# Cross attention on one Trainium2 core: value and query products split into three products of parts, and products ordered by their stationary operand

## The reference, cut to what matters

```python
x = layer_norm(x, ln_m_g, ln_m_b)             # the context, 4 x 512 x 128
lat = layer_norm(latents, ln_l_g, ln_l_b)     # the normed x, 4 x 256 x 128
q = lat @ Wq                                  # 16 heads of 64
kv = concatenate([x, lat], 1) @ Wkv           # 768 keys
k, v = split(kv)
attn = softmax(q @ k.T * scale)
return (attn @ v) @ Wout
```

## Time and profile before

| | us |
|---|---|
| median of 3 runs | 1062.45 |
| lowest, highest | 1061.57, 1063.77 |
| the profiled execution: its time | 1061.55 |
| the profiled execution: its span | 1059.4 |
| TensorE busy in the span (matmuls) | 979.9 |
| loads of stationary operands (PEld) | 800.9 |
| VectorE, ScalarE, GpSimd busy | 685.9, 573.2, 176.3 |

### The profile page before, as it was taken

The page is one execution under the profiler, slowest core; times in us unless marked ns, Lnnn a source line. Parts: engine busy times, 40 slices in busy tenths (PEclk is TensorE's granted clock), DMA queues, the critical chain, the costliest instruction groups (busy, mean ns, idle before and its releaser), DMA issues.

```text
span 1059.4 us, 22196 instructions
## 1 busy us (share of the span) xinstructions
PE 979.9 (92%) x7108; PEld 800.9 (76%) x7108; DVE 685.9 (65%) x1715; ACT 573.2 (54%) x1511; POOL 176.3 (17%) x291
## 2 busy tenths in 40 slices
PE   5899979999999999999997999979999888888888
PEld 3677768888888888888884877768999665555665
DVE  5878666556666555666635788853222699999673
ACT  3676556555555555555531677745444376666440
POOL 3434120000000000000002333200000234443100
PEclk9999989999999999999998999999999899999995
DMA  6000000000000000000000000010110000000000
GB/s 254 1 1 0 1 1 1 1 1 1 0 0 0 0 0 0 0 0 0 0 1 0 2 0 0 0 50 21 40 40 30 1 1 0 0 0 0 21 1 20
DMA packets 6402, 12.95 MB, mean 12 GB/s; under 512 B 480, under 2 KB 2528, under 8 KB 5984
## 3 DMA queue, kind: packets, MB, share of 16 engines
q1 hardware_dynamic: 6368, 12.51, 3.5%
HBM read 11.98 MB, written 0.52 MB: 12 GB/s over the span
## 4 chain that ended last, share of the span: by engine, by line
PE 77%; DVE 13%; issue 5%; ACT 2%; DVEq 1%; DMA 1%; POOL 1%; SPq 0%; ACTq 0%
PE psum L504 9%; PE psum L635 8%; PE psum L647 8%; PE psum L769 6%; PE psum L615 5%; PE psum L523 4%; PE psum L617 4%; PE psum L616 4%; PE psum L607 4%; DVE arena L1296 4%; PE psum L600 3%; PE psum L541 3%; DVE arena L1274 2%; PE psum L753 2%; PE psum L754 2%
## 5 line engine op out<-in xcount | busy, mean ns | idle before, releaser
L1419 DVE TENSOR_REDUCE xnegmax<-psum 128x1 f32<-128x768 f32 x128 | 122.4, 956 | 138.5 <-PE psum L617 138.2
L1075 ACT ACTIVATE arena<-psum,xnegmax 128x768 f32<-128x768 f32 x128 | 115.5, 903 | 138.5 <-DVE xnegmax L1419 97.4
L504 PE MATMUL psum<-arena 128*128 (+2 forms) x768 | 187.0, 359 | 1.6 <-ACT arena L970 0.3
L1726 POOL TENSOR_TENSOR arena<-arena,pack_a 128x256 f32 (+1 forms) x192 | 122.6, 647 | 145.6 <-PE psum L508 70.6
L970 ACT ACTIVATE arena<-psum,arena 128x256 f32<-128x256 f32 (+1 forms) x256 | 112.3, 446 | 57.1 <-PE psum L523 26.4
L523 PE MATMUL psum<-pack_a,arena 128*128 128x128 f32 x704 | 110.6, 277 | 29.9 <-ACT arena L977 23.9
L504 PEld LDWEIGHTS psum<-arena 128*128 128x128 f32 x768 | 122.3, 192 | 11.0 <-issue 4.4
L523 PEld LDWEIGHTS psum<-pack_a,arena 128*128 128x128 f32 x704 | 79.3, 141 | 57.9 <-issue 24.2
L635 PE MATMUL psum<-pack_a,arena 128*128 128x128 f32 x768 | 106.8, 275 | 0.2 <-ACT arena L1066 0.2
L615 PE MATMUL psum<-kv_high,xq_high 128*128 128x384 f32 x256 | 101.1, 395 | 1.7 <-DVE kv_low L1414 1.6
L1066 ACT ACTIVATE arena<-psum 128x512 f32<-128x512 f32 x128 | 75.9, 593 | 42.4 <-PE psum L635 42.4
(11 more groups left out here) (238 smaller groups left out, 1810.1 us busy)
## 6 DMA issues: line engine op xcount, KB each, us to landing
arena<-in_w SPq DMA_DIRECT2D x18, 256.0 KB, 2.8
pack_v<-in_pack_v SPq DMA_DIRECT2D x1, 1088.0 KB, 9.6
pack_l<-in_pack_l SPq DMA_DIRECT2D x1, 1079.5 KB, 12.5
pack_q<-in_pack_q SPq DMA_DIRECT2D x1, 1024.0 KB, 7.4
pack_a<-in_pack_a SPq DMA_DIRECT2D x1, 649.0 KB, 6.2
pack_f<-in_pack_f SPq DMA_DIRECT2D x1, 625.0 KB, 10.6
pack_b<-in_pack_b SPq DMA_DIRECT2D x1, 578.0 KB, 9.3
x<-in_x SPq DMA_DIRECT2D x2, 256.0 KB, 3.2
```

Source lines behind the costliest of these rows:

```text
L504: last = mm(bank[j][:, u * T:u * T + keys], qm[:, j, u * P:(u + 1) * P], kT[:, bass.ds(b * T, keys)], start=True, stop=not a.causal)
L1075: activation(xprob[:, u % 2, half * KEYS:(half + 1) * KEYS].rearrange("p (c w) -> p c w", c=2), src, ACT.Exp, bias=xnegmax[:, u % 2, half: ...
L1419: v.tensor_reduce(xnegmax[:, u % 2, half:half + 1], banks_pair(half), AX.XY, ALU.max, negate=True)\
L1726: pool.tensor_tensor(qm[:, j, :], qT[:, bass.ds(b * T, T)], headmask[:, bass.ds(g * HG + j, 1)].broadcast_to([P, T]), ALU.mult)\
```

## The change

Values and queries become three f32r products of parts instead of one f32 product. GpSimd makes the parts: acur_high and acur_low of each head's A, and wcur (two slots: high, low) of the pair's 128 columns of wv, once an iteration. In `values` the second and third product share their stationary operand. In `scores` the loops are exchanged: high x high for both banks, then high x low for both, then low x high for both, so that four products in a row have xq_high as their stationary operand and two have xq_low. Before the loop the first queries and values now need kv_high and kv_low of batch 0, so ScalarE makes kv_high of batch 0 ahead of the first xq_high, VectorE makes kv_low of batch 0 first of all, and the other three batches' low parts follow the copies of values. acur_low and wcur lie in the end of the arena, which the stage doesn't use.

```diff
                 def queries(it, u):
 
                     pe.wait_ge(sx["acur_ready"], it * 2 + u % 2 + 1)
-                    mm(bank[6][:, T:2 * T], acur[:, u % 2, :], kvT[:, u // 2, S2:KEYS], start=True, stop=True)\
+                    out, keys = bank[6][:, T:2 * T], slice(S2, KEYS)
+                    mm(out, acur_high[:, u % 2, :], kv_high[:, u // 2, keys], start=True, stop=False)
+                    mm(out, acur_high[:, u % 2, :], kv_low[:, u // 2, keys], start=False, stop=False)
+                    mm(out, acur_low[:, u % 2, :], kv_high[:, u // 2, keys], start=False, stop=True)\
                         .then_inc(sx["q_psum"], 1)
 
                 def values(it, b, half):
 
                     for k in range(3):
                         kt = 3 * half + k
-                        last = mm(bank[7][:, k * P:(k + 1) * P], kvT[:, b, kt * P:(kt + 1) * P],
-                                  wv[:, bass.ds(it * P, P)], start=True, stop=True)
+                        out, keys = bank[7][:, k * P:(k + 1) * P], slice(kt * P, (kt + 1) * P)
+                        mm(out, kv_low[:, b, keys], wcur[:, 0, :], start=True, stop=False)
+                        mm(out, kv_high[:, b, keys], wcur[:, 1, :], start=False, stop=False)
+                        last = mm(out, kv_high[:, b, keys], wcur[:, 0, :], start=False, stop=True)
                     last.then_inc(sx["v_psum"], 1)
 
                 def scores(u, half):
 
-                    for c in range(2):
-                        out, tile, keys = bank[2 * half + c][:, 0:W], slice(half * P, (half + 1) * P), slice(c * W, (c + 1) * W)
-                        mm(out, xq_high[:, u % 2, tile], kv_high[:, u // 2, keys], start=True, stop=False)
-                        mm(out, xq_high[:, u % 2, tile], kv_low[:, u // 2, keys], start=False, stop=False)
-                        last = mm(out, xq_low[:, u % 2, tile], kv_high[:, u // 2, keys], start=False, stop=True)
+                    tile = slice(half * P, (half + 1) * P)
+                    for i, (queries_part, keys_part) in enumerate(((xq_high, kv_high), (xq_high, kv_low), (xq_low, kv_high))):
+                        for c in range(2):
+                            last = mm(bank[2 * half + c][:, 0:W], queries_part[:, u % 2, tile],
+                                      keys_part[:, u // 2, c * W:(c + 1) * W], start=(i == 0), stop=(i == 2))
                     last.then_inc(sx["score_psum"], 1)
...
+                pe.wait_ge(sx["kv_split"], 1)
                 queries(0, 0)
+                pe.wait_ge(sx["wcur_ready"], 1)
...
-                            if not prev and not odd:
-
-                                pe.wait_ge(sx["kv_split"], b + 1)
                             scores(u, 0)
+                            if not prev and not odd and b + 1 < B:
+
+                                pe.wait_ge(sx["kv_split"], b + 2)
...
                             pe.wait_ge(sx["v_ready"], n + 2)
+                            if u == 6:
+
+                                pe.wait_ge(sx["wcur_ready"], it + 2)
                             values(it + (b + 1) // 4, (b + 1) % 4, odd)
...
-                act.wait_ge(sx["q_psum"], 1)
-                activation(xq_high[:, 0, :], bank[6][:, T:2 * T], ACT.Copy).then_inc(sx["q_high"], 1)
...
                 for b in range(B):
+                    if b == 1:
+                        act.wait_ge(sx["q_psum"], 1)
+                        activation(xq_high[:, 0, :], bank[6][:, T:2 * T], ACT.Copy).then_inc(sx["q_high"], 1)
...
+                key_low(0)
                 query_low(1, 0)
                 values(1, 0, 0)
                 values(2, 0, 1)
-                for b in range(B):
+                for b in range(1, B):
                     key_low(b)
...
             def cross():
+                wv, exact = col("v", "wv"), weff[:, :].rearrange("p (i c) -> p i c", i=3)
+
+                def weights(it, prev):
+
+                    if prev:
+
+                        pool.wait_ge(sx["v_psum"], it * 8)
+                    chain.did(pool.tensor_copy(exact[:, 2, :], wv[:, bass.ds(it * P, P)]))
+                    link(pool.tensor_copy(wcur[:, 0, :], wv[:, bass.ds(it * P, P)]))
+                    pool.tensor_tensor(wcur[:, 1, :], exact[:, 2, :], wcur[:, 0, :].bitcast(f32), ALU.subtract)\
+                        .then_inc(sx["wcur_ready"], 1)
+
                 def pair(it, prev):
                     for u in range(2):
                         if prev:
 
                             pool.wait_ge(sx["q_psum"], it * 8 - 1 + u)
-                        pool.tensor_copy(acur[:, u, :], A_flat[:, bass.ds(it * 2 * P + u * P, P)])\
+                        now = A_flat[:, bass.ds(it * 2 * P + u * P, P)]
+                        chain.did(pool.tensor_copy(exact[:, u, :], now))
+                        link(pool.tensor_copy(acur_high[:, u, :], now))
+                        pool.tensor_tensor(acur_low[:, u, :], exact[:, u, :], acur_high[:, u, :].bitcast(f32), ALU.subtract)\
                             .then_inc(sx["acur_ready"], 1)
 
                 pool.wait_ge(prep_act, 5)
                 pair(0, False)
+                pool.wait_ge(loaded["v"], 16)
+                weights(0, False)
                 with pool.Fori(1, XP + 1) as it:
+                    chain.enter(it, 1, 6)
+                    weights(it, True)
                     pair(it, True)
```

More of the change, by code:

```diff
@@ L137, in decoder @@
         ARENA = 17920
+        CROSS = 17408
+        with nc.sbuf_tensor("before_acur_low", [P, CROSS], f32), nc.sbuf_tensor("acur_low", [P, 2, P], f32r) as acur_low, \
+                nc.sbuf_tensor("wcur", [P, 2, P], f32r) as wcur:
+            pass
         arena = sb("arena", [P, ARENA])
@@ L175, in decoder @@
         xprob = area(2, 2 * KEYS)
+        assert area.at <= CROSS
         xq_high = sb("xq_high", [P, 2, T], f32r)
         xq_low = sb("xq_low", [P, 2, T], f32r)
-        acur = sb("acur", [P, 2, P])
+        acur_high = sb("acur_high", [P, 2, P], f32r)
         xnegmax = sb("xnegmax", [P, 2, 2])
@@ L327, in family @@
             return {n: sem(f"{tag}_{n}") for n in names}
-        sx = family("x", "zT_psum", "zT_act", "zT_dve", "acur_ready", "q_psum", "q_high", "q_ready", "kv_high",
+        sx = family("x", "zT_psum", "zT_act", "zT_dve", "acur_ready", "wcur_ready", "q_psum", "q_high", "q_ready", "kv_high",
                     "kv_split", "v_psum", "v_ready",
@@ L593, in cross @@
                 pe.wait_ge(loaded["v"], 16)
-                wv, wo = col("v", "wv"), col("v", "wout")
+                wo = col("v", "wout")
                 W = KEYS // 2
@@ L1698, in _ @@
         def _(pool):
-            done = [0]
+            chain = Chain(pool_chain)
             def link(instruction):
-                instruction.then_inc(pool_chain, 1)
-                done[0] += 1
-                pool.wait_ge(pool_chain, done[0])
+                chain.did(instruction)
+                chain.wait(pool)
             def rstd_jobs(keys):
@@ L1765, in cross @@
                 pair(0, False)
+                pool.wait_ge(loaded["v"], 16)
+                weights(0, False)
                 with pool.Fori(1, XP + 1) as it:
+                    chain.enter(it, 1, 6)
+                    weights(it, True)
                     pair(it, True)
-            pool.memset(half[:, :], -0.5).then_inc(pool_chain, 1)
-            done[0] += 1
-            pool.wait_ge(pool_chain, 1)
+                    chain.leave(XP)
+            link(pool.memset(half[:, :], -0.5))
             rstd_jobs(FIRST_JOBS)
```

## The result

The changed kernel takes 1074.91 us (median of 4 runs, 1073.38 to 1076.55) against 1062.82 (median of 4, 1061.57 to 1063.77): ratio 1.0115, 95% interval 1.0093 to 1.0137. It is slower by 12.1 us; the forecast was 9.6 slower. The profiled execution took 1076.17 us with a span of 1074.4.

The account below looks back on a forecast made before the run. TensorE was taken to bound the stage at full clock, with waits on the exponential's chain in the even half; 32 pairs x 0.25 = +8.0 us and +1.6 before the loop gave +9.6, 1072.0 us, range 1062 to 1081.

Parts of the forecast that it names:

- Values, +0.33 a unit by the load: In `values`, nine load-bound products at 0.111 us replace six such steps: 1.00 us against 0.67, +0.33 us a unit.
- Queries, -0.08: In the queries, three f32r products of 0.116 us take 0.35 in place of 0.43: -0.08 us a unit.
- The order in `scores`, zero: Exchanging the loops of `scores` changes nothing, since streaming (0.174 us) outlasts the load (0.111): zero.
- Where these fall: Odd half of a unit pair grows by 0.25 us; even half's waits absorb its extra work: 32 x 0.25 = +8.0.
- GpSimd, zero: Making wcur once an iteration takes near 1.2 us on GpSimd, within some 6.5 us of cover: zero.
- Before the loop, +1.6, bound 4: Ahead of the loop, the first queries wait for kv_high and kv_low of batch 0: +1.6 us, bounds 0 and 4.
- a spared load: In `values`, the second product on the same kv_high tile needs no new load: 1061.4 us; no-change rivals together 0.09.
- rival (b): In `values`, loads hidden better, about 81 ns a product: 0.73 us, total near 1063.4; no-change rivals together 0.09.
- The faster case: In `values`, loads don't bound and passes decide: 9 x 0.058 = 0.52 us, total 1056.8; chance 0.06.
- the narrow penalty: Narrow f32r value products cost 0.222 us each: total 1136, or near 1197 with slow queries too; chance 0.04.

Follow-up runs that it names:

- narrow stream: The changed kernel with the nine value products of a unit streaming 64 columns in place of 128: 1075.72 us, ratio to before 1.0122.
- half load: The changed kernel with the stationary operand of the nine value products 64 keys wide in place of 128: 1059.07 us, ratio to before 0.9963.

## Why the prediction was right

The direction, the main sum and its reasons held; one term was too small. Of the 12.1 us between the medians the pairs are 7.9, as forecast within 0.1, and 4.2 are left where 1.6 were forecast.

- *Values, +0.33 a unit by the load.* Right in kind, shown from both sides by the narrow stream and the half load. The size was 0.30 in the odd half. Against the run with values back to f32, it is 0.36 longer from the first value load to the first transpose there (1.03 against 0.67), and 0.05 shorter over the eight transposes (0.83 against 0.88).
- *Queries, -0.08.* 0.08 and 0.07 when undone next to values in parts, 0.05 next to f32 values. Slightly less than forecast.
- *The order in `scores`, zero.* Right.
- *Where these fall.* This was the choice that made the forecast 9.6 and not 18. The even half was forecast at 3.78 and is 3.79; the odd half at 8.85 and is 8.85; the pair at 12.63 and is 12.64. 31 pairs cost 7.9, as 32 x 0.25 = 8.0 said.
- *GpSimd, zero.* Right: 1.08 us of 6.5.
- *Before the loop, +1.6, bound 4.* This is the term that was mis-sized: 5.1 to 5.2 in the profiles (179.6 less the 174.5 of the run with the old start, and 5.5 less the 0.3 of the stages ahead), 1.7 to 3.1 by the medians of that run, 2.7 by the run with f32 values. The queries' delay came nearly as forecast (2.2 - 0.3 = 1.9). But the first scores loaded at 155.3, not at 153 to 154. The term took the queries' delay for the whole cost and left the rest to its upper bound of 4, which the profiles even pass. What it named for that bound, work at 1.2 GHz, came in every profile with the changed start, at one of two lengths: in the changed kernel TensorE, idle for 2.86 us, then worked nine-product groups at half clock until nearly 164, where a step is 0.21 instead of 0.11. Three more low parts on VectorE held the first maximum as well (158.72 against 154.75).
- The spans of the two profiles differ by 15.0 us (1074.4 and 1059.4): 5.5 up to the first `factors`, 7.9 in the pairs, and 1.6 in the stages behind, where no code differs. How the 4.2 that the medians leave beside the pairs divide between the start and the stages behind, no run shows.

Of the rivals, a spared load is out (a load for each product in the trace, the third of a tile 0.11 behind the second like the others). The price of some 0.08 us a product, that of rival (b), does not hold for these four-byte products: they step by 0.11, and the measurement decides. The faster case, at 0.06, and the narrow penalty, at 0.22, are out by the same steps. The Trainium skill, "TensorE: Matmul & The Clock Gate", section "LDWEIGHTS (loading the stationary operand)", gives the time of a load as its columns divided by 1.2 GHz, by an estimate from that formula 107 ns for 128. The step of 0.11 at 128 columns and full clock agrees, and 0.06 at 64 doesn't contradict it. At half clock the step was 0.21, which the formula, with no term for the clock's state, doesn't give.

## What to carry to other kernels

Count a matmul by the longer of load and stream, not by passes: splitting an f32 product of 128 columns into three f32r products trades two steps of 0.11 us for three and loses, while at 256 columns the stream outlasts the load (three steps of 0.12 for two of 0.21) and the same split gains a little. Before spreading a cost over a loop, cut the loop at each wait: half of an iteration can take in a quarter of a microsecond for nothing, and that same room can be filled with work moved from the other half. A start that lets TensorE stand idle can pay twice, once for the idle time and once for the work behind it at half clock, and the second price differs from execution to execution: here some 7 or 14 us at half clock behind the same start. Forecast such a term as a range, not as the wait alone.

## What the runs showed of the hardware that was not expected

The stages behind cross attention, which no run changes, varied by some 5 us between two profiles of the same kernel. Busy times from the last `factors` to the end, the changed kernel first and its second profile then:

```profile
571.80:1074.40 502.60, 449.09 (x3108) 351.98 (x3108) 334.26 (x998) 267.25 (x708) 118.22 (x184) 0.95 0.04 12
```

```profile
571.70:1069.30 497.60, 441.15 (x3108) 347.58 (x3108) 334.12 (x998) 267.71 (x708) 118.13 (x184) 0.96 0.04 12
```

The same 3108 matmuls, the same work on VectorE and ScalarE, and 5.0 us less with a granted clock of 0.96 instead of 0.95. So a single profile can't settle a difference of 5 us in this kernel's total. The mean length of a half can settle one of 1: it repeats to 0.01 us in the four profiles whose pairs should be alike (3.80, and 8.85 to 8.86), and 0.01 us in each of 31 pairs is 0.3.
